# Graph attention with residual norm: the first four heads' weights transposed in 32x32 squares on VectorE and through DRAM, the other eight on TensorE

## What is computed

```python
q = (x @ Wq.T).reshape(B, N, 12, 32);  k, v likewise (v has a bias bv)
a = einsum('bnhd,bmhd->bhnm', q, k) * 384**-0.5 + adj[:, None]
a = softmax(a, -1)           # rows that are all zero are masked out
o = einsum('bhnm,bmhd->bnhd', a, v).reshape(B, N, 384)
x = layernorm(x + o @ Wo.T + bo)
```

## Time and profile before

| | us |
|---|---|
| median of 3 runs (850.81 to 851.41) | 851.3 |
| the profiled execution | 852.93 |
| its span, first to last instruction | 850.9 |
| PE busy in the span | 826.5 (97%) |
| ACT busy | 645.2 (76%) |
| DVE busy | 557.8 (66%) |
| POOL busy | 454.6 (53%) |
| share of the 16 DMA engines taken by the kernel's transfers | 18.6% |

### The profile page before, as it was taken

How to read it: one execution, slowest core, us unless ns; L and a number is a source line. 1 busy time by engine, 2 the same in 40 slices (tenths; PEclk the granted TensorE clock), 3 DMA queues, 4 the chain that set the end, 5 groups by cost and what they waited for, 6 DMA issues and landing times.

```text
span 850.9 us, 27334 instructions
## 1 busy us (share of the span) xinstructions
PE 826.5 (97%) x8504; PEld 715.3 (84%) x8504; DVE 557.8 (66%) x2152; ACT 645.2 (76%) x2055; POOL 454.6 (53%) x518
## 2 busy tenths in 40 slices
PE   7999999999999999999999999999999999999974
PEld 6888888888888888888888888888888888888853
DVE  3666676766666676667676667676667676667672
ACT  3677787877787877777877777887777787777782
POOL 4455545655545655545655545665454665454522
PEclk8999999999999999999999999999999999999996
DMA  6211221211221111222111222111222110211010
GB/s 198 70 44 40 70 70 52 66 39 47 68 68 55 62 47 39 68 68 66 51 53 33 68 68 68 49 55 31 68 68 68 49 61 25 68 50 51 21 39 37
DMA packets 40864, 49.30 MB, mean 58 GB/s; under 512 B 2176, under 2 KB 40832, under 8 KB 40832
## 3 DMA queue, kind: packets, MB, share of 16 engines
q1 hardware_dynamic: 40832, 48.90, 18.6%
HBM read 36.31 MB, written 12.58 MB: 57 GB/s over the span
## 4 chain that ended last, share of the span: by engine, by line
PE 95%; ACT 1%; DVE 1%; issue 1%; POOL 1%; DMA 1%; SPq 0%; ACTq 0%; POOLq 0%; DVEq 0%
PE bank_b L487 41%; PE t_bank L578 21%; PE bank_a L615 11%; PE s_bank L564 10%; PE bank_a L487 8%; PE bank_a L592 2%; ACT prob L395 1%; DMA w_f<-in_wkT 1%; DVE neg L724 0%; PE bank_a L623 0%; POOL o_lo L303 0%; ACT y_out L428 0%; DVE probT L736 0%; POOL kq_lo L294 0%; DVE y L803 0%
## 5 line engine op out<-in xcount | busy, mean ns | idle before, releaser
L395 ACT ACTIVATE prob<-neg,negmax 128x256 f32<-128x256 f32 x768 | 379.8, 499 | 2.9 <-DVE negmax L724 2.8
L724 DVE CUSTOM_DVE_ANT_0 neg<-s_bank,bias 128x256 f32<-128x256 f32 x768 | 281.0, 419 | 39.0 <-PE s_bank L564 37.7
L578 PE MATMUL t_bank<-ident,prob 128*128 128x128 f32 x1536 | 207.4, 278 | 2.8 <-ACT prob L395 2.8
L578 PEld LDWEIGHTS t_bank<-ident,prob 128*128 128x128 f32 x1536 | 169.0, 140 | 41.3 <-ACT prob L395 18.6
L406 ACT ACTIVATE probT<-t_bank 128x512 f32<-128x512 f32 x192 | 113.4, 591 | 105.5 <-PE t_bank L578 105.5
L312 POOL COPY inv_wide<-inv 128x768 f32<-128x768 f32 x32 | 26.4, 824 | 250.3 <-DVE inv L784 250.3
L395 ACT ACTIVATION_READ_ACCUMULATOR prob<-neg,negmax 128x1 f32 x768 | 146.9, 191 | 0.0
L736 DVE COPY probT<-t_bank 128x512 f32<-128x512 f32 x192 | 131.6, 685 | 1.3 <-PE t_bank L578 1.2
L294 POOL TENSOR_TENSOR kq_lo<-kq,kq_hi 128x512 fp32r<-128x512 f32 x96 | 123.6, 1287 | 7.7
L487 PE MATMUL bank_b<-xt_hi,w_hi 128*128 128x256 f32 x378 | 112.7, 298 | 0.0
L487 PE MATMUL bank_b<-xt_lo,w_hi 128*128 128x256 f32 x378 | 107.0, 283 | 0.0
(11 more groups left out here) (70 smaller groups left out, 1738.6 us busy)
## 6 DMA issues: line engine op xcount, KB each, us to landing
xt<-in_xT SPq DMA_DIRECT2D x32, 384.0 KB, 3.5
xr<-in_x SPq DMA_DIRECT2D x32, 384.0 KB, 3.1
out_y<-y_out SPq DMA_DIRECT2D x32, 384.0 KB, 2.5
bias<-in_adj SPq DMA_DIRECT2D x32, 256.0 KB, 2.7
w_f<-in_wkT SPq DMA_DIRECT2D x3, 192.0 KB, 4.0
w_f<-in_wqT SPq DMA_DIRECT2D x1, 576.0 KB, 6.0
w_f<-in_wvT SPq DMA_DIRECT2D x1, 576.0 KB, 7.8
w_f<-in_woT SPq DMA_DIRECT2D x1, 576.0 KB, 10.2
```

What stands on the lines that cost most here:

```text
L395: nc.scalar.activation(prob[:, u % PROB_RING, k], neg[:, h, w.c], ACT.Exp, scale=-1.0, bias=negmax[t.p][:, w.c, h:h + 1], accum_out=sums[t ...
L578: last = nc.tensor.transpose(t_bank[u % 2][:, k, m, :], prob[:, u % PROB_RING, k, P * m:P * (m + 1)], ident[:])
L724: nc.vector.tensor_tensor_reduce(out=neg[:, h, w.c], in0=s_bank[h % JH][:, w.c, :], in1=bias[t.p][:, w.c, :], scale=-1.0, scalar=BIG, op0= ...
```

## The change

- Units 0 to 3 (group 0) no longer go through PE. `square(t, u)` on DVE turns each 32x32 square of the unit's weights by one instruction of 512 elements per partition, SBUF to SBUF, with the columns taken at a stride of four, into a staging area in `w_f`. When the four units are there, SP stores the staging area (128 partitions of 8 KB, 1 MB) to a scratch tensor in DRAM, waits for it, and loads it back in another arrangement (pieces of 2 KB, 1 MB) into `sq_probT`. `weigh(t, 0)` reads that tile in runs of 32 columns.
- Only units 4 to 11 are transposed on PE and copied to `probT`; the copies that go away are those of units 0 and 2 on DVE, 1 and 3 on ACT. `probT` now has a place for each of its heads.
- The order is written anew on all three engines. `weigh` goes 1, 0, 2 instead of 0, 1, 2: `weigh(t, 1)` stands ahead of K01, `weigh(t, 0)` behind units 8 and 9. `scores(t, 1)` stands where units 0 and 1 stood. Y0 goes behind `weigh(t, 0)`. On DVE `invert` and `add_bias(t + 1, 0)` go to the end of the step, both `moments` go ahead of the squares. On ACT `exps(t + 1, 0)` goes to the end of the step, and Q12 is read out behind `exps(t, 5)` instead of `exps(t, 3)`.

The core of the diff:

```diff
+    def weighed(self, g):
+        return self.count(KC, WEIGHED.index(g) + 1)      # WEIGHED = (1, 0, 2)
...
+                if t.attend:
+                    sp.wait_ge(squared, t.count(GROUP_UNITS, GROUP_UNITS))
+                    sp.dma_start(sq_dram, sq_stage.rearrange("p b h m c s -> p b (h m c s)")
+                                 ).then_inc(sq_stored, DMA)
+                    sp.wait_ge(sq_stored, t.count(DMA, DMA))
+                    sp.dma_start(sq_probT[:].rearrange("p i h m c s -> p i (h m c s)"),
+                                 sq_dram.rearrange("(i r) b n -> (r b) i n", i=P // SQ)).then_inc(sq_loaded, DMA)
...
             def weigh(t, g):
-                copied(t, [u for u in range(4 * g + 4) if u in ON_DVE][-1])
-                copied(t, [u for u in range(4 * g + 4) if u not in ON_DVE][-1])
                 if g == 0:
+                    pe.wait_ge(sq_loaded, t.count(DMA, DMA))
+                else:
+                    copied(t, 4 * g + 2)
+                    copied(t, 4 * g + 3)
...
+            def square(t, u):
+                w = Unit(u)
+                dve.wait_ge(prob_ready, t.count(H * NT, PAIR * (u + 1)))
+                if u == 0 and (t.looped or t.c >= 1):
+                    dve.wait_ge(sq_stored, t.count(DMA))
+                a = w.heads[0]
+                nc.vector.transpose(sq_stage[:, :, a:a + PAIR, :, w.c].rearrange("p b h m s -> p (h m) b s"),
+                                    prob[:, u % PROB_RING].rearrange("p k (m r b) -> p (k m) b r", m=NT, b=P // SQ)
+                                    ).then_inc(squared, 1)
...
 (PE's order in a step)
                 if t.finish:
                     weigh(t.before(), 2)
                 if t.attend:
-                    transposes(t, 0)
-                    transposes(t, 1)
+                    scores(t, 1)
                 if t.project:
                     unit(t, "Q12")
                 if t.finish:
                     spread(t, 0)
                 if t.attend:
-                    scores(t, 1)
-                    transposes(t, 2)
-                    transposes(t, 3)
-                if t.finish:
-                    spread(t, 1)
-                if t.project:
-                    unit(t, "V0")
-                if t.attend:
-                    weigh(t, 0)
                     transposes(t, 4)
                     transposes(t, 5)
...
+                if t.finish:
+                    spread(t, 1)
+                if t.project:
+                    unit(t, "V0")
+                if t.attend:
                     transposes(t, 6)
                     transposes(t, 7)
+                    scores(t, 2)
+                if t.project:
+                    unit(t, "V1")
+                if t.attend:
+                    weigh(t, 1)
                 if t.project:
                     unit(t, "K01")
-                if t.finish:
-                    unit(t, "Y0")
                 if t.attend:
                     transposes(t, 8)
                     transposes(t, 9)
-                    weigh(t, 1)
+                    weigh(t, 0)
+                if t.finish:
+                    unit(t, "Y0")
```

More of the change, by code:

```diff
@@ L25 @@
 PROB_RING = 4
-PT_RING = 2 * JH
+GROUP_UNITS = NT * JH // PAIR
 WARM_START = 24
 DMA = 16
-ON_DVE = (0, 2, 4, 6, 8, 10)
+ON_PE = tuple(range(GROUP_UNITS, UNITS))
+ON_DVE = (4, 6, 8, 10)
+WEIGHED = (1, 0, 2)
 class Unit:
@@ L72, in copies, with turned @@
     def copies(self, u, on_dve):
-        mine = [k for k in range(UNITS) if (k in ON_DVE) == on_dve]
+        mine = [k for k in ON_PE if (k in ON_DVE) == on_dve]
         return self.count(len(mine), len([k for k in mine if k <= u]))
-    def unit(self, u):
-        return (self, u) if u >= 0 else (self.before(), u + UNITS)
+    def turned(self, u):
+        return self.count(len(ON_PE), u - GROUP_UNITS + 1)
+    def weighed(self, g):
+        return self.count(KC, WEIGHED.index(g) + 1)
 def steps(eng, body):
@@ L436, in step @@
                     w_hi_part(W_O)
+                    exps(t.after(), 0)
                     return
@@ L444, in step @@
                     save_kq(t, "K2Q0")
+                if t.attend:
+                    exps(t, 2)
                 if t.finish:
@@ L461, in step @@
                 if t.attend:
-                    save_o(t, 0)
-                    exps(t, 6)
-                    copy_probT(t, 5)
                     exps(t, 7)
+                    copy_probT(t, 7)
                 if t.before().finish:
@@ L469, in step @@
                 if t.attend:
-                    copy_probT(t, 7)
                     exps(t, 8)
+                    save_o(t, 1)
+                    exps(t, 9)
+                    exps(t, 10)
                 if t.project:
@@ L474, in step @@
                 if t.attend:
-                    exps(t, 9)
-                    exps(t, 10)
                     copy_probT(t, 9)
-                    save_o(t, 1)
+                    save_o(t, 0)
                     exps(t, 11)
+                if t.after().attend:
+                    exps(t.after(), 0)
             steps(act, step)
@@ L817, in step @@
                     w_lo_part(W_V)
+                    add_bias(t.after(), 0)
                     return
@@ L820, in step @@
                     residual(t.before(), 1)
-                if t.attend:
-                    add_bias(t, 0)
                 if t.finish:
                     copy_probT(t.before(), 10)
+                if t.first:
+                    save_v(t.before(), 0)
+                    save_v(t.before(), 1)
+                    w_lo_part(W_O)
                 if t.attend:
@@ L828, in step @@
                     add_bias(t, 3)
-                if t.first:
-                    save_v(t.before(), 0)
-                    save_v(t.before(), 1)
-                    w_lo_part(W_O)
-                if t.finish:
-                    invert(t)
                 if t.before().finish:
+                    moments(t.before(), 0)
                     moments(t.before(), 1)
                 if t.attend:
-                    copy_probT(t, 0)
+                    square(t, 0)
+                    square(t, 1)
+                    add_bias(t, 4)
+                    square(t, 2)
+                    add_bias(t, 5)
+                    square(t, 3)
                 if t.finish:
@@ L865, in step @@
                 if t.attend:
-                    copy_probT(t, 8)
-                if t.finish:
-                    moments(t, 0)
-                if t.attend:
                     read_flag(t)
                     mask(t)
+                    invert(t.after())
+                if t.after().attend:
+                    add_bias(t.after(), 0)
             steps(dve, step)
```

99 lines of the change are left out of this document (58 added, 41 removed).

## The result

The changed kernel takes **1013.3 us** (1011.3 to 1014.9, four runs) against 851.05 us for the kernel of before in the same session: ratio **1.1905** (95% interval 1.1883 to 1.1927). The forecast was 899 with a range of 862 to 955: right in sign, far outside in size. The profiled span is 1013.1 us, 162.2 more than before.

A forecast was written before the change was run, and what follows sets the result against it. PE was taken to bound the kernel: 97% busy, its chain all PE without waits. Terms -1.8 + 2.7 + 0.6 + 0.05 = +1.55 us a step, over 31 steps +48 on 851.3, gave 899 us; range 862 to 955.

The forecast's parts named there:

- Two pairs off PE, -1.8: Units 0 to 3 leave PE, two pairs with their switches to and from other products: 1.8 us a step less.
- 2.7 us of waits before unit 7: PE waits for exps in the step's first half: 1.1 before unit 5, 0.25 before unit 6, 1.40 before unit 7.
- K01 behind `weigh`, +0.6: K01 overwrites `bank_a` directly behind `weigh(t, 1)`, so PE idles for the read-out: 0.6 us a step more.
- The sum, +1.55: All terms of a step together: 1.55 us longer, in 31 steps +48 us, giving 899 us.
- The square at 0.62: Each of four DVE squares a step takes 0.62 us, judged by a 512-element copy at 0.60 start to start.
- The rival of dear squares: DVE squares take 1.29 us each, 2.7 us a step more: 982 us; chance 0.08.
- The transfers, nothing: Scratch store (4.5 us) and load (5.1 us) finish about 2 us ahead of `weigh(t, 0)`, at no cost.
- The clock: Rival: the new waits drop PE's clock to half for 3.4 us, losing 1.7; once a step 952 us; chance 0.10.
- PE idle before unit 5 and 7 and before K01: Sign: PE idles 1.1 and 1.4 us before the transposes of units 5 and 7, 0.6 before K01's first matmul.
- The load ahead of `weigh(t, 0)`: Sign: the load of `sq_probT` has landed 2 us ahead of `weigh(t, 0)`.
- DVE without idle from `residual` to `divide`: Sign: in the step's first half DVE works from `residual` to `divide` without any idle time.
- PEclk leaves 9 in the middle: Sign of error: the forecast is wrong if PE's clock reading leaves 9 in the middle of the trace.

The follow-up runs named there:

- the repaired kernel: Changed kernel with squares reading 32 neighbouring columns, four scratch loads for one, and 16 semaphore increments first in VectorE's queue; order kept: 908.5 us, ratio 1.066.
- the 16 increments in the changed kernel: Changed kernel with 16 semaphore increments put once into VectorE's queue, ahead of the first unit's bias: 956.1 us, ratio 1.123.
- the shifted kernel of before: Kernel of before with 14 semaphore increments put once into VectorE's queue, ahead of the first unit's bias: 910.8 us, ratio 1.070.

## Why the prediction was wrong, point by point

| from | to | us | measured by |
|---|---|---|---|
| before | the change with short squares, body in two pieces | 851.4 to 908.5: +57 | the repaired kernel |
| short squares | squares at a step of 16 bytes | 908.5 to 956.1: +48 | the 16 increments in the changed kernel, which also has one load for four |
| two pieces | three pieces of code | 956.1 to 1013.3: +57 | the same against the changed kernel |

- **Two pairs off PE, -1.8.** Right. Before's six pairs of units take 5.42 us of a step from start to start, 0.90 each. In the repaired kernel the two pairs that don't wait take 0.88 and 0.96; what the two that wait cost beyond that is the next point.
- **2.7 us of waits before unit 7.** Right in place and nearly in size. Start to start, units 4 and 5 take 1.78 us for the 0.93 of the pair in their place before (+0.85, forecast 1.1), V0 1.93 for 1.76 (+0.17, forecast 0.25), units 6 and 7 2.28 for 0.85 (+1.43, forecast 1.4): 2.45 in all. The idle entries, 0.64 and 1.04, are smaller than what they cost, since a stretch that is waited on also shows the end of its last matmul as busy.
- **K01 behind `weigh`, +0.6.** Right: from `weigh(t, 1)` to K01 1.58 us for 1.00, idle 0.50, in all 31 steps (15.6 us).
- **The sum, +1.55.** The repaired kernel's steps are 1.6 to 1.7 us longer than before's. The waits come out a little smaller than the forecast; about 0.3 is spread over the switches of PE between products, which the walk left out. 899 was forecast for this kernel and 908.5 measured: about 50 of the 57 us are these steps, nearly 5 stand between the last two `flag` (26.04 us for 21.40, at a mean granted clock of 0.80 for 1.00; the runs don't separate the clock's part), and the rest at both ends.
- **The square at 0.62.** This term of the sum is the first step that failed. From start to start it is 1.02: 4 x 0.40 = 1.6 us a step, 50 us by that count and 48 measured. The nearest row, a copy of 512 elements, reads neighbouring elements; "with the columns taken at a stride of four" stood in my own description of the change and was given no price. The 0.62 was right for what the row showed: with neighbouring columns the square takes 0.63 from start to start, 0.70 busy against the copy's 0.69. The rival of dear squares named this step, at 1.29 for the measured 1.02, with a chance of 0.08.
- **No row for the jump.** The second step that failed, and the larger: no term and no rival spoke of where the loop's body lies. The trace of before held nothing that shows a fetch at the jump, but the program did show that VectorE's body grows from 269 instructions to 281, and the section of the Trainium skill on fetching, cited above, was there. Whether the jump stalls is partly luck: the same body 16 instructions further on doesn't stall, and before's body 14 further on does. The runs showed 57 us for it. Without it the change takes 956, a microsecond over my upper end.
- **The transfers, nothing.** Right. The store lands in 3.9 us (forecast 4.5), the load in 5.6 (5.1). Issued at 519.08, it is there at 524.7, and `weigh(t, 0)` starts at 527.47; taking the trip away changed nothing.
- **The clock.** It fell, and cost nothing. (In the repaired kernel, the one that the walk described, it stayed at 1.00 from 33 to 865 us.) In the short step above PE had waited 0.80 and 1.01, and then, in the middle of V0 and while the store ran, its clock was at the lower of the two levels. Stretches, columns as in the earlier trace rows: the fall, the short step that holds it, and a short step of the same kernel without one:

```profile
516.00:518.30 2.30, 2.30 (x9) 2.30 (x8) 1.82 (x10) 1.99 (x8) 2.23 (x2) 0.50 0.99 410
501.49:530.17 28.68, 26.32 (x250) 21.85 (x250) 19.89 (x69) 19.36 (x62) 14.24 (x16) 0.94 0.36 124
377.60:406.27 28.67, 25.06 (x250) 20.43 (x250) 19.89 (x69) 19.36 (x62) 14.25 (x16) 1.00 0.36 124
```

  28.68 with the fall, 28.67 at full clock throughout. With the loop written out, 12 of the 29 middle steps hold such a fall (granted clock 0.94) and 17 none, and all take 28.45 to 28.49. The slow matmuls filled time that PE would have spent waiting: ahead of unit 7 it idles 1.04 us in the step at full clock, and with the fall units 6 and 7 follow one another without a wait (x8):

```profile
395.52 0.66 PE L622 MATMUL t_bank<-ident,prob 128*128 128x128 f32 x4 [1.04 <-ACT prob L436]
518.77 1.31 PE L622 MATMUL t_bank<-ident,prob 128*128 128x128 f32 x8
```

  The waits of 0.80 and 1.01 stand in both steps, so they alone don't bring the fall about. The rival's price, 1.7 a step, forgot that a slow engine in front of a wait loses only what exceeds the wait.
- **Signs named ahead.** PE idle before unit 5 and 7 and before K01: seen in the repaired kernel, 0.64, 1.04 and 0.50. The load ahead of `weigh(t, 0)`: seen, by 2.8 us. DVE without idle from `residual` to `divide`: broken at its first two instructions, by the wait behind the jump. PEclk leaves 9 in the middle (two eights), which I had named as a sign of error; it wasn't the cause.

## What to carry to other kernels

Count VectorE's instructions in a loop's body before and after an edit, waits and register instructions included. Where the body comes to touch three of the fetched blocks, the jump back can cost microseconds: 4.8 to 5.0 us a turn here. A handful of idle instructions ahead of the loop shows within one run whether it does. Price an access by its stride as well as by its element count. And work taken from a saturated engine only counts in an order that puts other work between a producer's last step and its reader: here the same edit was 19% slower as written, 7% slower with the first two mended, and 3% faster with all three.

## What the runs showed of the hardware that I had not expected

- A VectorE transpose of 32x32 float32 squares, 512 elements per partition: 0.70 us busy with elements 4 or 8 bytes apart, 1.10 us at 16 bytes.
- 14 instructions without work, once, ahead of the loop: 851 to 911 us. Behind each jump VectorE's next instruction came after 3.4 to 3.6 us (2.8 to 3.0 in the changed kernel, 0.3 where two pieces hold the body), and then it stood still for another 1.8.
- 224 semaphore increments in a row took VectorE 20.2 us, 0.09 each.
- The granted clock can fall for 3 us in a step and leave the step's length as it was.
- The steps of the loop differ in turn, 25.36 and 25.45 in the kernel of before, 28.55 and 28.70 in the changed one with 16 increments. 0.09 of it stands between the transposes of units 10 and 11 and K2Q0: 0.98 us in the steps that follow a jump, 0.89 in the others, and 0.81 in all steps when the loop is written out.
- Left open: the other 0.06 us of that difference in the changed kernel, and why the first instruction behind the jump comes after 3.4 us in the shifted kernel of before and after 2.8 in the changed one. (Its idle entry there, 4.67, also holds the 1.1 us between DVE's last work and the jump.) Neither was tried.
